# Graph attention and mixture kernel: how the table of edge counts is built from 36 columns of edges at a time

## The chip, the cores and the metric

The kernel runs on one core of a Trainium2 chip. The metric is the device time of one execution in microseconds, the median of several runs. PE is the matrix engine (TensorE), DVE the vector engine, ACT the scalar engine, POOL is GpSimd and SP the engine whose queue issues the DMAs.

## The reference, cut to what matters

There are 1250 nodes and 41250 edges, sorted by their destination. Two layers of graph attention with a residual are followed by a soft mixture of experts. Only the first part matters here:

```
e     = leaky_relu(a_src[src] + a_dst[dst])        # for each edge and head
alpha = softmax of e over the edges of one dst
out   = segment_sum(alpha * h[src], dst)            # 8 heads, then relu
```

The kernel doesn't gather edges. It counts how often each edge (dst, src) occurs, `count[dst, src]`, takes the logarithm of the counts once, and does the attention of each head as a dense one over all sources: `exp(e + ln count)`, normalised by row. So the reference's sums over edges become a 1250 x 1250 table and ordinary matrix products.

## The kernel before, in words

The work is a chain of blocks, each ended by a barrier of all engines. Three of them matter here.

`constants` fills identity, iota and others by POOL.

`first_stage` normalises x, makes h and its attention values (matrix products, 10 tiles of 128 nodes), and finds for each of the 10 tiles of destinations which columns of 128 edges belong to it (`bounds_of_tiles`). Then comes the counting, from line 683 on: for each destination tile `j` a loop over groups of `GROUP` = 36 columns, which with this data runs once for each tile, so ten groups in all. A group has 6 pieces (`b`) of 6 columns (`i`). For each column of 128 edges two one-hot matrices are needed:

- `one_dst`, 128 edges x 128 destinations of this tile, the stationary operand. ACT makes 33 of the 36 (line 782, `apart` = |iota - dst| column by column; line 787, `one_dst` = relu(1 - apart) for a whole piece), DVE the other 3 (line 616).
- `one_src`, 128 edges x 625 sources, the moving operand. Each column counts both halves of the sources at once, since an edge into the upper half is worth `RADIX` = 6144 instead of 1. DVE makes all 36 (line 618).

PE multiplies them into a PSUM accumulator (line 876, two products of 512 and 113 columns for each column of edges). A ring of three pieces couples the engines: DVE and ACT wait for `free` before they write piece b, PE waits for `src_ready`, `dst_ready` and `own_ready`.

The accumulator of a group is unpacked in the middle of the next group. ACT's `round_off` (lines 741 and 745) finds the upper count, `above`, ahead of its piece 3; DVE's `unpack` (lines 627, 629, 632) follows ahead of DVE's piece 3 and adds both halves to `number`. After the group of tile j, ACT takes `log(j - 1)` (line 753) into the one buffer `lns`, for which it waits until DVE's `finish(j - 2)` (line 637) has read the logarithms before. DVE does after the group of tile j: `second_weights` (line 600, for j from 1 to 8), `finish(j - 2)`, and `clear` (line 641), a memset of the `number` buffer that the tile after needs. Three clears stand ahead of the first group as well.

`attend_heads` works through 80 steps (8 heads x 10 tiles) of softmax (ACT, DVE, POOL), transposition and product with h (PE). The product is divided by the softmax's sum. The sums stand in a column and are needed along a row, so `turn_inverse` (lines 951 to 961) has SP write the inverses to DRAM (line 954) and read them back spread over all partitions (line 960), for each of 24 chunks; DVE's `divide` (line 1056) waits for it.

Of the kernel before, what the change touches and what calls it, by code (L numbers as in the profile page):

```python
# [24 lines left out]
F32 = mybir.dt.float32  # L25
F16 = mybir.dt.float16
# [4 lines left out]
ds = bass.ds  # L31
# [207 lines left out]
def constants(nc, mem, sem):  # L239
# [4 lines left out]
    one = mem("one", [P, 1], F32)  # L244
    eps = mem("eps", [P, 1], F32)
# [4 lines left out]
    with nc.Block() as block:  # L250

        @block.gpsimd
        def _(eng):
            eng.memset(ident[:, :], 0.0).then_inc(filled, 1)
            eng.memset(picks[:, :, :], 0.0).then_inc(filled, 1)
            eng.memset(one[:, :], 1.0).then_inc(made, 1)
            eng.memset(eps[:, :], 1e-5).then_inc(made, 1)
# [11 lines left out]
            eng.wait_ge(made, 7)  # L269

    return {"ident": ident, "picks": picks, "one": one, "eps": eps, "none": none, "iota": iota, "zeros": zeros}


def first_stage(nc, mem, early, sem, const, rows, edges, w1t, att1, w2t, att2, bias, h, nad, a_rows, s_row, in_s,
# [13 lines left out]
    ON_DVE = (1, 0, 1, 0, 1, 0)  # L288
    ETP = ET + GROUP
    MOST = NT * -(-ET // GROUP)  # L290
    assert len(ON_DVE) == PIECES and PIECES % RING == 0
# [17 lines left out]
    lns = mem("lns", [P, N], F32)  # L309
    rounded = mem("rounded", [P, HALF], F32)  # L310
# [27 lines left out]
    dst = mem("dst", [P, ETP], F32)  # L338
# [3 lines left out]
    down = mem("down", [P, ET], F16)  # L342
    tiles = mem("tiles", [P, NT], F16)
# [8 lines left out]
    minus_dst = mem("minus_dst", [P, ETP], F32)  # L352
# [15 lines left out]
    row_ready, bounds_ready, minus_ready, levels = (  # L368
        sem("fs_row"), sem("fs_bounds"), sem("fs_minus"), sem("fs_levels"))
    src_ready, apart_ready, dst_ready, own_ready, free = (  # L370
        sem("fs_src"), sem("fs_apart"), sem("fs_dst"), sem("fs_own"), sem("fs_free"))
# [6 lines left out]
    with nc.psum_tensor("fs", [P, 8, BANK], F32) as banks, nc.Block() as block:  # L378
# [26 lines left out]
        def place(b, i):  # L405


            return ((b + 1) % RING) * PIECE + i

# [53 lines left out]
        def _(eng):  # L463
            eng.memset(level[:, :], LEVEL[0]).then_inc(levels, 1)
# [8 lines left out]
            eng.wait_ge(levels, 2)  # L473

        @block.vector
        def _(eng):
            full = [P, NT, ET]

            def tiles_of_edges():
                eng.memset(src[:, ET:ETP], float(NO_NODE)).then_inc(pads, 1)  # L480
                eng.memset(minus_dst[:, ET:ETP], -float(NO_NODE)).then_inc(pads, 1)
# [21 lines left out]
            def nodes_of_edges():  # L503
# [3 lines left out]
                eng.wait_ge(pads, 4)  # L507
                eng.tensor_scalar(upper[:, :], src[:, 0:ET], float(HALF), None, ALU.is_ge).then_inc(casts, 1)
                eng.tensor_scalar(minus_dst[:, 0:ET], dst[:, 0:ET], -1.0, None, ALU.mult).then_inc(minus_ready, 1)
# [4 lines left out]
                                         ALU.mult, ALU.add).then_inc(casts, 1)  # L514

# [106 lines left out]
            def unpack(g, tile):  # L622
# [3 lines left out]
                eng.wait_ge(above_ready, g + 2)  # L626
                eng.scalar_tensor_tensor(rest[:, :], above[:, :], -RADIX, counts(g + 2), ALU.mult, ALU.add)\
# [7 lines left out]
            def finish(j):  # L635
                eng.wait_ge(ln_ready, j + 1)
                eng.scalar_tensor_tensor(ln_c[:, j, 0:N], lns[:, :], NONE_TIMES, lns[:, :],
                                         ALU.mult, ALU.min).then_inc(out_ready, 1)

            def clear(tile):  # L640
                eng.memset(number[:, tile, :], 0.0).then_inc(cleared, 1)
# [41 lines left out]
            for tile in range(3):  # L683
                clear(tile)
            eng.wait_ge(cleared, 3)
            eng.memset(number[:, 0, 0:1], 0.0).then_inc(number_ready, 2)
            eng.wait_ge(casts, 7)
            for j, first, last, shift in spans(eng, True):
                with eng.Fori(first, last) as g:
                    at = first_column(g, shift)  # L690
# [17 lines left out]
                if 2 <= j < NT - 1:  # L708
                    clear((j - 2) % 3)
# [1394 lines left out]
```

## Time and profile before

| what | us |
|---|---|
| median of 3 runs | 1834.65 (1834.17 to 1835.0) |
| the profiled execution's own time | 1835.22 |
| its span, first to last instruction | 1833.4 |
| PE busy | 1634.2 (89%) |
| DVE busy | 1113.2 (61%) |
| ACT busy | 840.0 (46%) |
| POOL busy | 264.2 (14%) |

The counting lies between 106 and 340 us of the span. All times below are us from the span's start, unless they are durations. In a timeline row the columns are start, duration, engine, line, operation, output and inputs, and in square brackets the idle time of the engine before it with what ended it; x5 means five merged instructions.

### The profile page before, as it was taken

The numbers are of one execution on the slowest core, as the hardware profiler recorded it, in microseconds if no ns is written. First come the engines' busy times: TensorE is split into PE (matmuls) and PEld (weight loads), VectorE is DVE, ScalarE is ACT, GpSimd is POOL, SyncE is SP. The second block draws the span as 40 slices with busy tenths as digits, with TensorE's granted clock in tenths as the row PEclk, the third lists the DMA queues.
The fourth block names the chain that finished last, engine by engine and source line by source line (L and its number), as shares of the span: only waits on it lengthen the run. The fifth ranks groups of instructions, "written<-read, shape, count | busy, mean of one in ns | idle before, by whom it ended". The sixth has DMA issues, their size and how long they took to land. (4 is left out here: it accounts for less than half of the span.)

```text
span 1833.4 us, 27161 instructions
## 1 busy us (share of the span) xinstructions
PE 1634.2 (89%) x9537; PEld 956.7 (52%) x9537; DVE 1113.2 (61%) x1853; ACT 840.0 (46%) x1298; POOL 264.2 (14%) x118
## 2 busy tenths in 40 slices
PE   6877665499999989999998999999999969998999
PEld 3433222266656546545553566555565636665555
DVE  7989888689999746332232555555555556665301
ACT  2268777688888638211111333333333335554200
POOL 0000000577878423000000000000000000000000
PEclk9988888699999989999998999999999989999999
DMA  4001000012212240211001111221112225441111
GB/s 168 18 27 48 19 18 10 1 35 48 34 30 36 19 149 1 83 64 35 35 18 36 65 65 64 68 68 68 68 68 68 68 98 176 148 147 30 61 62 49
DMA packets 49747, 108.57 MB, mean 59 GB/s; under 512 B 16638, under 2 KB 18776, under 8 KB 49532
## 3 DMA queue, kind: packets, MB, share of 16 engines
q1 hardware_dynamic: 49596, 107.38, 19.1%
q8 instruction: 49, 0.80, 0.2%
q14 instruction: 38, 0.31, 0.1%
q10 hardware_dynamic: 64, 0.08, 0.0%
HBM read 79.02 MB, written 28.43 MB: 59 GB/s over the span
## 5 line engine op out<-in xcount | busy, mean ns | idle before, releaser
L977 POOL TENSOR_TENSOR base<-s_row,ln_c 128x1250 f32<-128x1250 f32 x80 | 227.6, 2847 | 54.3 <-DVE top L1032 52.9
L876 PE MATMUL fs<-one_src,one_dst 128*128 128x512 f16 x720 | 132.3, 348 | 79.5 <-DVE one_src L618 41.1
L99 PE MATMUL di_l<-x2t_hi,ph_hi 128*128 128x512 f16 (+1 forms) x576 | 196.6, 341 | 5.2 <-POOL p L1594 3.8
L100 PE MATMUL di_l<-x2t_lo,ph_hi 128*128 128x512 f16 (+1 forms) x576 | 196.6, 341 | 0.0
L101 PE MATMUL di_l<-x2t_hi,ph_lo 128*128 128x512 f16 (+1 forms) x576 | 196.4, 341 | 0.0
L1101 PE MATMUL at_o<-pt,h 128*128 128x384 f32 (+1 forms) x480 | 185.9, 525 | 0.0
L876 PEld LDWEIGHTS fs<-one_src,one_dst 128*128 128x128 f16 x720 | 62.0, 113 | 148.6 <-ACT one_dst L787 75.5
L1088 PE MATMUL at_t<-ident,q 128*128 128x128 f32 x800 | 107.4, 283 | 35.7 <-ACT q L1011 35.0
L1088 PEld LDWEIGHTS at_t<-ident,q 128*128 128x128 f32 x800 | 92.2, 145 | 80.1 <-ACT q L1011 71.1
L1653 DVE SCALAR_TENSOR_TENSOR pt_lo<-di_t,pt_hi 128x1280 f16<-128x1280 f32 x32 | 47.7, 1492 | 140.6 <-ACT pt_hi L1607 140.6
L99 PE MATMUL co_c<-ps_hi,hid_hi 128*128 128x305 f16 (+1 forms) x384 | 114.8, 299 | 20.5 <-DVE ps_lo L1896 19.8
L618 DVE TENSOR_SCALAR one_src<-iota,src,worth 128x625 f16<-128x625 f16 x360 | 130.3, 437 | 3.0 <-issue 3.0
L987 ACT ACTIVATE at_r<-s_row,nad 128x1250 f32<-128x1250 f32 x80 | 104.5, 1307 | 37.7 <-DVE top L1032 36.6
L1032 DVE CUSTOM_DVE_ANT_0 q<-at_r,base 128x1250 f32<-128x1250 f32 x80 | 115.8, 1448 | 5.3 <-POOL base L977 3.6
L100 PE MATMUL co_c<-ps_lo,hid_hi 128*128 128x305 f16 (+1 forms) x384 | 114.6, 299 | 0.0
L101 PE MATMUL co_c<-ps_hi,hid_lo 128*128 128x305 f16 (+1 forms) x384 | 114.5, 298 | 0.0
L1101 PEld LDWEIGHTS at_o<-pt,h 128*128 128x128 f32 x480 | 86.0, 192 | 54.5 <-issue 23.8
L1041 DVE COPY pt<-at_t 128x512 f32<-128x512 f32 x160 | 103.1, 685 | 18.6 <-PE at_t L1088 17.3
L782 ACT ACTIVATE apart<-iota,minus_dst 128x128 f16<-128x128 f16 x330 | 102.2, 386 | 11.3 <-PE fs L876 8.7
L1011 ACT ACTIVATE q<-q,neg_top 128x1250 f32<-128x1250 f32 x80 | 105.9, 1324 | 0.8 <-DVE neg_top L1035 0.8
L99 PE MATMUL di_h<-xw,pt_hi 128*128 (+1 forms) x320 | 104.3, 326 | 1.8 <-DVE pt_lo L1653 1.8
L100 PE MATMUL di_h<-xw,pt_hi 128*128 (+1 forms) x320 | 104.3, 326 | 0.0
(271 smaller groups left out, 3305.4 us busy)
## 6 DMA issues: line engine op xcount, KB each, us to landing
logits_t<-lg SPq DMA_DIRECT2D x32, 625.0 KB, 3.6
logits_in<-logits_t SPq DMA_DIRECT2D x32, 625.0 KB, 4.7
phf<-in_phi SPq DMA_DIRECT2D x32, 384.0 KB, 3.9
w2f<-in_w2t SPq DMA_DIRECT2D x16, 384.0 KB, 3.6
s_row<-a_rows SPq DMA_DIRECT2D x9, 640.0 KB, 5.7
ew1f<-in_fw SPq DMA_DIRECT2D x6, 768.0 KB, 4.9
wf<-in_fw SPq DMA_DIRECT2D x12, 384.0 KB, 5.0
xs<-in_x SPq DMA_DIRECT2D x10, 384.0 KB, 4.2
```

The source lines that it names most:

```text
L99: eng.matmul(out, lh, rh, start=first, stop=False, skip_group_check=True)
L100: eng.matmul(out, lh, rl, start=False, stop=False, skip_group_check=True)
L101: return eng.matmul(out, ll, rh, start=False, stop=last, skip_group_check=True)
L618: eng.tensor_scalar(one_src[:, place(b, i), 0:HALF], const["iota"][:, 0:HALF], src[:, ds(col, 1)], worth[:, ds(col, 1)], ALU.is_equal, ALU ...
L876: mm = eng.matmul(counts(g)[:, a:a + n], one_dst[:, place(b, i), :], one_src[:, place(b, i), a:a + n], start=False, stop=b == PIECES - 1 a ...
L977: eng.tensor_tensor(base[:, k % 2, 0:N], s_row[:, head % 2, 0:N], ln_c[:, j, 0:N], ALU.add)\
L987: eng.activation(rp[:, 0:N], s_row[:, head % 2, 0:N], ACT.Relu, bias=nad[:, k:k + 1], scale=-0.8).then_inc(relu_ready, 1)
L1011: eng.activation(q[:, k % RING, 0:N], q[:, k % RING, 0:N], ACT.Exp, bias=neg_top[:, k:k + 1], accum_out=den[:, k:k + 1]).then_inc(p_ready, 1)
L1032: eng.tensor_tensor_reduce(q[:, k % RING, 0:N], rp[:, 0:N], base[:, k % 2, 0:N], 1.0, -MASK / 2, ALU.add, ALU.max, top[:, k:k + 1]).then_i ...
L1041: eng.tensor_copy(pt[:, k % NT, b * (BANK // P):(b + 1) * (BANK // P), :] .rearrange("p t n -> p (t n)"), tp[:, b * BANK:(b + 1) * BANK]). ...
L1088: mm = eng.transpose(tp[:, t * P:(t + 1) * P], q[:, k % RING, t * P:(t + 1) * P], const["ident"][:, :])
L1101: mm = eng.matmul(op[:, g % 2, 0:n * P], h[:, head, t, :], pt[:, a:a + n, t, :], start=t == 0, stop=t == NT - 1, skip_group_check=True)
```

## The change

Counting: DVE makes all of `one_dst`, six columns in one instruction. `one_dst` is laid out `[P, ring, 128 destinations, 6 columns]`, so that a comparison of a constant `spread` (the destination's number, repeated six times) with six entries of `from_tile` fills a piece; PE then reads each column's stationary matrix with a step of 6 elements. `from_tile` is the destination less the tile's start, one small DVE instruction for each group. Of the 36 `one_src` columns of a group ACT makes 10 (`ON_ACT`), each by two instructions over 625 elements, |iota - src| and relu(worth - worth * apart); DVE makes the other 26. ACT's `round_off` moves from piece 3 to piece 2 and DVE's `unpack` from piece 3 to piece 4. `lns` has two buffers. The clears leave DVE: POOL does the first three during the products ahead, ACT the others, after the logarithm, as a Copy with scale 0.

Attention: for the last of the 24 chunks the inverse sums are spread by DVE, PE and ACT (a diagonal matrix multiplied by ones) instead of by SP's way through DRAM.

```diff
+    ones = mem("ones", [P, P], F32)                    # constants, filled by POOL
-    ON_DVE = (1, 0, 1, 0, 1, 0)
+    ON_ACT = (2, 2, 1, 2, 1, 2)
-    lns = mem("lns", [P, N], F32)
+    lns = mem("lns", [P, 2, N], F32)
-    one_dst = mem("one_dst", [P, RING * PIECE, P], F16)
-    apart = mem("apart", [P, 2, PIECE, P], F16)
+    one_dst = mem("one_dst", [P, RING, P, PIECE], F16)
+    apart = mem("apart", [P, 2, HALF_PADDED], F16)
+    spread = mem("spread", [P, P, PIECE], F16)
+    from_tile = mem("from_tile", [P, GROUP], F16)
...
+            eng.wait_ge(casts, 7)                          # POOL
+            for tile in range(3):
+                eng.memset(number[:, tile, :], 0.0).then_inc(cleared, 1)
...
-                eng.tensor_scalar(minus_dst[:, 0:ET], dst[:, 0:ET], -1.0, None, ALU.mult).then_inc(minus_ready, 1)
+                eng.tensor_scalar(minus_src[:, :], src[:, :], -1.0, None, ALU.mult).then_inc(minus_ready, 1)
+                eng.tensor_scalar(minus_worth[:, :], worth[:, :], -1.0, None, ALU.mult).then_inc(minus_ready, 1)
...
             def rows_of(j, g, at, b):                     # DVE
                 eng.wait_ge(free, PIECES * g + b + 1)
-                for i in range(PIECE):
+                eng.tensor_tensor(one_dst[:, ring(b), :, :], spread[:, :, :],
+                                  from_tile[:, b * PIECE:(b + 1) * PIECE].unsqueeze(1)
+                                  .to_broadcast([P, P, PIECE]), ALU.is_equal).then_inc(dst_ready, 1)
+                for i in range(PIECE - ON_ACT[b]):
                     col = at + (b * PIECE + i)
-                    if i >= PIECE - ON_DVE[b]:
-                        eng.tensor_scalar(one_dst[:, place(b, i), :], const["iota"][:, j * P:(j + 1) * P],
-                                          dst[:, ds(col, 1)], None, ALU.is_equal).then_inc(own_ready, 1)
...
-            for tile in range(3):
-                clear(tile)
...
+                    eng.tensor_scalar(from_tile[:, :], dst[:, ds(at, GROUP)], -float(j * P), None, ALU.add)\
+                       .then_inc(from_ready, 1)
-                        if b == PIECES // 2:
+                        if b == 4:
                             eng.wait_ge(cleared, 3 + max(j - 2, 0))
                             unpack(g - 1, tile_of(j, g, first))
...
-                if 2 <= j < NT - 1:
-                    clear((j - 2) % 3)
...
             def log(j, g):                                # ACT
                 eng.wait_ge(number_ready, 2 * g + 4)
-                if j >= 1:
-                    eng.wait_ge(out_ready, j)
+                if j >= 2:
+                    eng.wait_ge(out_ready, j - 1)
...
+                if j + 3 < NT:
+                    eng.wait_ge(ln_ready, j + 1)
+                    eng.activation(number[:, j % 3, :], number[:, j % 3, :], ACT.Copy, scale=0.0)\
+                       .then_inc(cleared, 1)
...
-                        if b == PIECES // 2:
+                        if b == 2:
                             round_off(g - 1)
...
+                        for i in range(PIECE - ON_ACT[b], PIECE):
+                            k = sum(ON_ACT[0:b]) + i - (PIECE - ON_ACT[b])
+                            col = at + (b * PIECE + i)
+                            eng.wait_ge(act_ready, sum(ON_ACT) * g + (k + 1 if k else 2))
+                            eng.activation(apart[:, k % 2, 0:HALF], const["iota"][:, 0:HALF],
+                                           ACT.Abs, bias=minus_src[:, ds(col, 1)]).then_inc(apart_ready, 1)
+                            eng.wait_ge(apart_ready, sum(ON_ACT) * g + k + 1)
+                            eng.activation(one_src[:, place(b, i), 0:HALF], apart[:, k % 2, 0:HALF],
+                                           ACT.Relu, bias=worth[:, ds(col, 1)],
+                                           scale=minus_worth[:, ds(col, 1)]).then_inc(act_ready, 1)
...
-                                mm = eng.matmul(counts(g)[:, a:a + n], one_dst[:, place(b, i), :],
+                                mm = eng.matmul(counts(g)[:, a:a + n], one_dst[:, ring(b), :, i],
...
+                if k == STEPS:                             # attend_heads, ACT
+                    eng.wait_ge(inv_turned, 1)
+                    eng.wait_ge(divided, LAST - 1)
+                    eng.activation(inv[:, LAST % 2, 0:n * P], tp[:, 0:n * P], ACT.Copy).then_inc(inv_read, 1)
...
+                if k == STEPS:                             # DVE, for its n = 3 tiles
+                        eng.tensor_scalar(spread[:, i * P:(i + 1) * P], const["ident"][:, :],
+                                          factor[:, head * NT + a + i:head * NT + a + i + 1], None, ALU.mult)\
...
+                if k == STEPS + 1:                         # PE
+                        mm = eng.matmul(tp[:, i * P:(i + 1) * P], const["ones"][:, :], spread[:, i * P:(i + 1) * P],
+                                        start=True, stop=True)
```

## Rows read from the trace of the kernel before

**Rows 1.** One destination tile by windows: us busy and count by engine, PEclk, DMA.
```profile
197.70:220.20 22.50, 13.61 (x75) 6.65 (x75) 19.45 (x49) 17.64 (x43) 0.00 (x0) 0.80 0.06 19
```

**Rows 2.** Waits from 117 to 329 us: who for whom, total us, times, longest.
```profile
ACT lns L753 <- DVE ln_c L637: 31.1, 7, 4.5
DVE rest L627 <- ACT above L745: 20.3, 8, 3.1
```

**Rows 3.** Timeline of one destination tile, DVE and ACT.
```profile
220.01 1.57 ACT L782 ACTIVATE apart<-iota,minus_dst 128x128 f16<-128x128 f16 x5
...
221.47 4.34 DVE L618 TENSOR_SCALAR one_src<-iota,src,worth 128x625 f16<-128x625 f16 x12
221.61 0.83 ACT L787 ACTIVATE one_dst<-apart,one 128x640 f16<-128x640 f16 x1
...
227.38 0.67 ACT L741 ACTIVATE rounded<-fs 128x625 f32 x1
...
228.81 1.84 ACT L782 ACTIVATE apart<-iota,minus_dst 128x128 f16<-128x128 f16 x6
229.13 0.81 DVE L627 SCALAR_TENSOR_TENSOR rest<-above,fs 128x625 f32<-128x625 f32 x1 [2.82 <-ACT above L745]
...
231.30 3.98 DVE L618 TENSOR_SCALAR one_src<-iota,src,worth 128x625 f16<-128x625 f16 x11
...
237.82 0.95 DVE L600 CUSTOM_DVE_ANT_0 unread<-w2f,attb 128x768 f16<-128x768 f32 x1
...
241.13 1.34 ACT L753 ACTIVATE lns<-number,none 128x1250 f32<-128x1250 f32 x1 [4.47 <-DVE ln_c L637]
```

**Rows 4.** Groups of ACT instructions by form: busy us and mean ns, idle before.
```profile
L782 ACT ACTIVATE apart<-iota,minus_dst 128x128 f16<-128x128 f16 x330 | 102.2, 386 | 11.3 <-PE fs L876 8.7 <-issue 1.8 <-PE fs L857 0.4
L787 ACT ACTIVATE one_dst<-apart,one 128x640 f16<-128x640 f16 x30 | 24.8, 828 | 1.0
L745 ACT ACTIVATE above<-rounded 128x625 f32<-128x625 f32 x11 | 8.0, 726 | 1.4
```

**Rows 5.** DVE two-input instructions on f16 (lines 491, 496): ns min/median/max.
```profile
L491 DVE TENSOR_TENSOR within<-dst_tile,tiles x1: 3532/3532/3532, 26.8 to 26.8; 128x3240 f16<-128x3240 f16 x1
L496 DVE TENSOR_TENSOR ranks<-within,up x1: 1794/1794/1794, 37.8 to 37.8; 128x3240 f16<-128x3240 f16 x1
```

**Rows 6.** Loads of the stationary operand, lines 876 (f16) and 1101 (f32).
```profile
L876 PEld LDWEIGHTS fs<-one_src,one_dst x720: 95/98/152, 117.0 to 329.0; 128*128 128x128 f16 x180
L1101 PEld LDWEIGHTS at_o<-pt,h x480: 190/190/338, 363.7 to 639.6; 128*128 128x128 f32 x160
```

**Rows 7.** Timeline of the start of the counting.
```profile
106.33 1.57 ACT L782 ACTIVATE apart<-iota,minus_dst 128x128 f16<-128x128 f16 x5 [1.43 <-issue]
...
107.26 2.29 DVE L590 TENSOR_REDUCE a_all<-weighted 128x16 f32<-128x2048 f32 x1
...
111.56 0.78 PE L852 MATMUL fs<-level,minus_level 128*128 128x512 f16 x4
...
115.67 1.86 DVE L618 TENSOR_SCALAR one_src<-iota,src,worth 128x625 f16<-128x625 f16 x5 [2.00 <-issue]
```

**Rows 8.** Timeline of the end of the counting and the start of the next block.
```profile
329.88 1.34 ACT L753 ACTIVATE lns<-number,none 128x1250 f32<-128x1250 f32 x1 [2.68 <-DVE ln_c L637]
...
332.86 0.81 DVE L627 SCALAR_TENSOR_TENSOR rest<-above,fs 128x625 f32<-128x625 f32 x1 [3.08 <-ACT above L745]
...
336.57 1.34 ACT L753 ACTIVATE lns<-number,none 128x1250 f32<-128x1250 f32 x1 [3.93 <-DVE ln_c L637]
...
339.93 0.21 ACT L1004 ACTIVATE bias_act<-bias_col 128x8 f32<-128x8 f32 x1 [2.02 <-PEq L378]
```

**Rows 9.** Timeline of the end of the attention over the heads.
```profile
629.24 11.13 PE L1101 MATMUL at_o<-pt,h 128*128 128x384 f32 x34
...
640.50 0.32 SPq L960 DMA_DIRECT2D inv<-inv_rows  x1
...
644.97 0.57 DVE L1056 TENSOR_TENSOR at_o<-at_o,inv 128x384 f32<-128x384 f32 x1 [3.60 <-DMA inv<-inv_rows]
```

More of the change, by code:

```diff
@@ L268, in _ @@
                               channel_multiplier=0).then_inc(made, 1)
-            eng.wait_ge(made, 7)
-    return {"ident": ident, "picks": picks, "one": one, "eps": eps, "none": none, "iota": iota, "zeros": zeros}
+            eng.wait_ge(made, 8)
+    return {"ident": ident, "picks": picks, "one": one, "ones": ones, "eps": eps, "none": none, "iota": iota, "zeros": zeros}
 def first_stage(nc, mem, early, sem, const, rows, edges, w1t, att1, w2t, att2, bias, h, nad, a_rows, s_row, in_s,
@@ L408, in place, with ring @@
             return ((b + 1) % RING) * PIECE + i
+        def ring(b):
+            return (b + 1) % RING
         def tile_of(j, g, first):
@@ L463, in _ @@
         def _(eng):
+            eng.iota(spread[:, :, :], [[1, P], [0, PIECE]], base=0, channel_multiplier=0,
+                     allow_small_or_imprecise_dtypes=True).then_inc(levels, 1)
             eng.memset(level[:, :], LEVEL[0]).then_inc(levels, 1)
@@ L636, in finish @@
                 eng.wait_ge(ln_ready, j + 1)
-                eng.scalar_tensor_tensor(ln_c[:, j, 0:N], lns[:, :], NONE_TIMES, lns[:, :],
+                eng.scalar_tensor_tensor(ln_c[:, j, 0:N], lns[:, j % 2, :], NONE_TIMES, lns[:, j % 2, :],
                                          ALU.mult, ALU.min).then_inc(out_ready, 1)
-            def clear(tile):
-                eng.memset(number[:, tile, :], 0.0).then_inc(cleared, 1)
             def low_w1(k):
@@ L681, in _ @@
                     bounds_of_tiles()
-            for tile in range(3):
-                clear(tile)
-            eng.wait_ge(cleared, 3)
-            eng.memset(number[:, 0, 0:1], 0.0).then_inc(number_ready, 2)
             eng.wait_ge(casts, 7)
+            eng.wait_ge(levels, 3)
+            eng.memset(from_tile[:, 0:1], 0.0).then_inc(dst_ready, 1)
             for j, first, last, shift in spans(eng, True):
@@ L770, in _ @@
                     deviation(t + 3)
-            eng.wait_ge(minus_ready, 1)
+            eng.wait_ge(minus_ready, 2)
+            eng.activation(apart[:, 0, 0:1], const["one"][:, 0:1], ACT.Copy).then_inc(act_ready, 2)
             for j, first, last, shift in spans(eng, True):
@@ L776, in _ @@
                     for b in range(PIECES):
-                        if b == PIECES // 2:
+                        if b == 2:
                             round_off(g - 1)
                         eng.wait_ge(free, PIECES * g + b + 1)
-                        n = PIECE - ON_DVE[b]
-                        for i in range(n):
-                            eng.activation(apart[:, b % 2, i, :], const["iota"][:, j * P:(j + 1) * P],
-                                           ACT.Abs, bias=minus_dst[:, ds(at + (b * PIECE + i), 1)])\
-                               .then_inc(apart_ready, 1)
-                        eng.wait_ge(apart_ready, (GROUP - sum(ON_DVE)) * g
-                                    + (PIECE * (b + 1) - sum(ON_DVE[0:b + 1])))
-                        eng.activation(one_dst[:, place(b, 0):place(b, n), :], apart[:, b % 2, 0:n, :],
-                                       ACT.Relu, bias=const["one"][:, 0:1], scale=-1.0).then_inc(dst_ready, 1)
+                        for i in range(PIECE - ON_ACT[b], PIECE):
[8 more added lines that the diff above has]
+                                           scale=minus_worth[:, ds(col, 1)]).then_inc(act_ready, 1)
                 if j == 0:
@@ L846, in _ @@
             eng.wait_ge(h_read, NT - 1)
[L847 removed]
+            eng.wait_ge(levels, 3)
             eng.wait_ge(bounds_ready, 2)
```

78 lines of the change are left out of this document (54 added, 24 removed).

## The prediction

> **What bounds the kernel now.** I read the page first for the busy shares (PE 89% over the span), which mislead here: the change lies in a stretch in which PE has gaps. So the windows of one destination tile come next [rows 1]. A tile takes 22.5 us, PE is busy for 13.6 of them at a granted clock of 0.80 (between its two levels, 1.2 and 2.4 GHz), DVE for 19.5 and ACT for 17.6. No engine is full, so two of them wait for each other in turn. The waits name them [rows 2]: ACT's logarithm waits 31.1 us for DVE's `finish` in 7 tiles, and DVE's `unpack` waits 20.3 us for ACT's `above`. The timeline shows one round [rows 3]. DVE ends `second_weights` and `finish` 241.13 - 0.10 - 237.82 = 3.2 us after the start of the former; only then may ACT take the logarithm, after 4.47 us of idleness, since `lns` is one buffer. ACT so starts the next tile's `one_dst` late and reaches `round_off` late, and DVE stands idle for 2.82 us ahead of `unpack`. The tile is a ring over both engines: ACT's work of 22.5 - 4.5 = 18.0 us and 4.5 us of DVE.
>
> **ACT after the change.** The prices are [rows 4]. An activation of 128 columns takes 386 ns and one of 640 columns 828, both with a bias read per partition, so 0.863 ns a column, and 386 + 497 x 0.863 = 815 ns for 625 columns. Without such an operand 625 columns take 726 ns [rows 4], so an operand costs about 89. The new |iota - src| has one (815 ns); the new relu has two, bias and scale; no row has two, so it lies between 815 and, with the price of the first paid again, 904. I take 904, as the first operand is the nearest row. Between instructions: five in 1.57 us [rows 3] is (1.57 - 0.386) / 4 = 296 ns from start to start, so neighbours that don't depend overlap by 90 ns. A dependent one starts 221.61 - 221.58 = 0.03 us after the end of what it needs, that of `apart` and `one_dst` [rows 3]. `round_off`, two dependent instructions with one more wait, takes 228.81 - 227.38 = 1.43 us, which leaves 1.43 - 0.67 - 0.73 + 0.09 = 0.12 between them. The new pair is built like `apart` and `one_dst`: 0.815 + 0.03 + 0.904 - 0.09 = 1.66 us. Bounds: 1.57 if the second operand is free, 1.76 if each pair has the gap of 0.12.
>
> A tile on ACT is then 10 x 1.66 = 16.6, `round_off` 1.43, the logarithm 1.34 - 0.09 = 1.25, the clear (0.726 + 625 x 0.000863 = 1.27 us, dependent on the logarithm, so 1.27 + 0.03 - 0.09 = 1.2) and 0.1 for the loop's end: 20.6 us. The 33 + 6 instructions that made `one_dst` are gone. The clear is 1.2 us that ACT didn't have.
>
> **DVE after the change.** A `one_src` costs 4.34 / 12 = 0.36 us [rows 3], 26 of them 9.4. The comparison has 768 elements. Two rows bracket it [rows 5]: 3240 elements took 1794 ns where the repeated input runs along its last dimension (0.52 ns an element and 0.11), and 3532 where one input stands still along it (1.04 and 0.16). In the new comparison both inputs run along the last dimension, of 6 elements, and repeat over the one before, as in the first of these rows, though with an inner run of 324 there and 6 here. So 0.51 us, 0.42 net of the overlap, 2.5 for six; by the other row 0.87 net and 5.2. `VectorE: DVE Perf Modes` of the Trainium skill, section "Mode 2×_1P", asks for 16-bit operands with a step of one and says nothing of a long run; by it the first row holds; the two rows agree with it so far, and no row has a run of 6. With 0.4 for `from_tile` and its waits (at most a `one_src`, 0.44), `unpack` 231.30 - 229.13 = 2.2 and the 3.2 above, DVE's tile is 17.7 us (20.4 by the other row). Either way it is below ACT's 20.6. The comparisons, and the clear and the three `one_dst` that leave DVE, therefore lie beside ACT's work and count for nothing in the steady state; if ACT were faster, DVE's 17.7 would be next.
>
> **The waits.** ACT's logarithm now waits for a `finish` one tile further back, done some 20 us before. `round_off` stands behind four pairs, 6.6 us into ACT's tile, so `above` is there after 8.1. DVE reaches `unpack` after 0.4 + 4 x 0.42 + 17 x 0.36 = 8.2 us of its own; behind the waiting `unpack` are its pieces 4 and 5, which PE needs only when ACT's pairs of them are done, 14.7 and 18.0 us into the tile. ACT itself waits only for `free`: for its piece 3, at 6.6 + 1.4 + 1.7 = 9.7 us, PE must have done piece 0, whose last pair was ready at 3.3. PE needs 625 columns for each column of edges, 0.52 us at 1.2 GHz and 0.26 at 2.4, 18.8 or 9.4 us a tile, so 3.1 us a piece at most. It keeps up at either level, and its clock matters only after the last pair. `round_off`'s and `unpack`'s new waits for `number_ready` are for an unpack a tile earlier: nothing.
>
> **The stationary operand** is read with a step of 12 bytes. No row has such a load; the nearest take 98 ns (f16) and 190 (f32) [rows 6]. I take 98 to 190: at 190 ns the loads add at most 0.1 us to each column at 1.2 GHz, 36 x 0.62 = 22 us, at 2.4 GHz 36 x 0.40 = 14.5, and the busier PE gets the higher level for part of the tile, so still nothing but up to 0.6 us at the end.
> `SBUF — State Buffer` of the skill, "Specifications", speaks against the change: lines are of 16 bytes and want two hits each for full bandwidth. A step of 12 bytes has 1.3 hits. It gives no price; were it the ratio 2 / 1.33, a load would by my estimate take 0.15 us, which ACT's tile still covers. The last rival has its extreme.
>
> **The walk.** ACT starts on the pairs at 106.33 [rows 7] as now, plus 0.3 for two more small DVE instructions in the stage ahead, which I charge in full (each at most 0.44), and 0.1 for a fill of 128 columns in `constants`: 106.7. DVE's three clears and the 2.00 us of issue behind them [rows 7] leave the path: DVE can begin at 107.26 + 2.29 = 109.6 instead of 115.67, PE at 111.56 + 0.78 = 112.3, so neither holds ACT, whose piece 2 is due at 106.7 + 8.1. Tile 0 ends on ACT at 106.7 + 18.0, and the read of h adds up to 1.3: 126.0. Tiles 1 to 7 at 20.6 end at 270.2, tile 8 without a clear at 289.6, tile 9's pairs at 307.6. PE's last piece takes 1.6 to 3.1 more: 310.0. Now from `round_off` on: before, it could start 1.25 after the logarithm of 329.88, at 331.12, and the next block began at 339.93, 8.8 us later [rows 8]. In these, the logarithm of the last tile waited 336.57 - 335.10 = 1.5 for a `finish`, which two buffers remove: 7.3. The next block begins at 317.3 instead of 339.9, 22.6 us earlier.
>
> **The end of the attention.** Before, the last chunk's product was done at 629.24 + 11.13 = 640.4, but the last inverses came at 644.97, for SP issued their load only at 640.50 [rows 9]. After, PE carries three more f32 products of 128 columns in this stretch. Its 34 instructions in 11.13 us are 0.33 each with 384 columns; six with 128 columns lie between a third of that and all of it, 0.65 to 2.0 us, and I take 1.2, as a load of 190 ns each can't be hidden [rows 6]. The division starts at 641.6, 3.4 us earlier. DVE's three small products and ACT's copy stand while PE works on the chunks before. What is late next is PE's product itself.
>
> **Sum.** 22.6 + 3.4 = 26.0 from the profiled execution's 1835.2 is 1809.2; the median of the runs lies 0.6 lower: 1808.6, so 1809.
>
> **Rivals.** (1) The forecast: ACT's pairs set the pace, 1809; chance 0.72. Its own bounds: pairs of 1.57 or 1.76 move 100 of them by -9 or +10, so 1800 to 1819. For it speaks that each length is from a row of the same engine and type.
> (2) DVE sets the pace, chance 0.13. If short runs cost the comparison its double rate, DVE's tile is 20.4, as long as ACT's, and each wait of one on the other adds: 0.6 us a tile for ten tiles, 1815. The start and end gains stay. Against it stands the first row of [rows 5].
> (3) ACT pays more for a dependent pair or for finding its addresses, chance 0.09: a whole 0.2 us for each of 100 pairs, 1829. For it: each pair now has three addresses taken from a register; the 2.00 us of issue in [rows 7] show that an engine's sequencer can be the slow part. Against: `apart` and DVE's `one_src` ran with such addresses at 0.30 and 0.36.
> (4) On the other side, chance 0.06: PE's strided loads. The load isn't hidden beside a product of 113 columns. The change loses once a tile takes 22.5 + 7/10 = 23.2 us (the 7 us being won at both ends), so once a column takes 0.64: a load of 0.21 us more than now at 1.2 GHz, or 0.38 at 2.4. The longest load in the rows is 0.338 [rows 6]; with it added at 1.2 GHz the tile is 36 x (0.52 + 0.24) = 27.4 us, ten of them 49 us more than now less 7, so 1877. Against it: PE has 8.9 us of gaps a tile now and is still granted 0.80 [rows 1]; without gaps it should be granted no less.
> That the edit doesn't work as told (ACT still waiting for DVE) would show as 1 us a tile and lies within (2)'s region.
>
> **Chances and range.** Measurement tells 0.2% (3.7 us) from no change. (1) to (3) are all faster: 0.93; 0.02 for the stretch between 1831 and 1838, which only a mild form of (4) reaches; slower 0.05. The range is 1800 to 1823: the bounds of (1), all of (2) with the ACT bound on top of it; (3) and (4), 0.15, stay outside.
>
> **What would show it.** Right: a tile of about 20.6 us in the windows; ACT over 19 us busy in it and without idle time of a microsecond; pairs of 0.82 and 0.90 us; no row of `log` waiting for `finish`; the comparison at 0.51 us; the counting's block ending near 317; the last `divide` waiting for PE and no DMA. Wrong: a comparison near 0.96; a relu above 1 us, or gaps ahead of `apart`; PE's load above 0.2 us with both others waiting for `free`; idle time of ACT ahead of `round_off`, which would mean that PE comes late.

## The result, and the profile after

| | before | after |
|---|---|---|
| median of 4 runs each, us | 1834.41 (1833.85 to 1835.0) | 1823.41 (1822.06 to 1824.34) |
| the profiled execution's own time | 1835.22 | 1823.05 |
| its span | 1833.4 | 1821.3 |
| one destination tile | 22.50 | 21.78 |
| first pair (or `apart`) of ACT starts | 106.33 | 109.40 |
| the attention's block begins | 339.93 | 332.61 |
| the step behind the attention begins | 649.19 | 637.24 |

The ratio is 0.9939 (95% interval 0.9922 to 0.9957): faster by 11.0 us, where 26 were forecast. Of the 12.1 us between the two spans 7.3 come from the counting and 4.6 from the attention; what follows takes 1184.2 us before and 1184.1 after. The shares of the page, each with the engine's busy us, its part of the span and its instructions:

```profile
PE 1635.9 (90%) x9543; PEld 962.7 (53%) x9543; DVE 1094.6 (60%) x1786; ACT 860.8 (47%) x1117; POOL 270.6 (15%) x124
```

The windows of three neighbouring destination tiles of the changed kernel, with the columns of [rows 1]:

```profile
197.46:219.22 21.76, 13.31 (x76) 6.85 (x75) 17.63 (x42) 20.06 (x24) 0.00 (x0) 0.91 0.06 19
219.22:241.00 21.78, 15.34 (x74) 7.18 (x73) 17.66 (x42) 20.07 (x25) 0.00 (x0) 0.74 0.07 20
241.00:262.78 21.78, 13.46 (x81) 7.08 (x79) 17.65 (x42) 20.07 (x24) 0.00 (x0) 0.96 0.06 18
```

The ring over two engines is gone. The tile takes 21.8 us whether PE is granted 0.74 or 0.96, DVE is busy for 17.65 and ACT for 20.07. The rest of ACT's time isn't a wait for another engine, as its waits between 100 and 325 us show (who for whom, total us, times, longest):

```profile
ACT apart L807 <- issue: 3.5, 8, 1.4
ACT apart L807 <- PE fs L902: 1.2, 1, 1.2
```

No row of the logarithm waiting for `ln_c` is left [rows 2]. So ACT sets the pace, as forecast, and its tile is 1.2 us longer than the 20.6 of the forecast. Where that lies is in ACT's timeline, one pair and a tile's end:

```profile
199.23 0.80 ACT L807 ACTIVATE apart<-iota,minus_src 128x625 f16<-128x625 f16 x1
...
200.17 0.91 ACT L810 ACTIVATE one_src<-apart,worth,minus_worth 128x625 f16<-128x625 f16 x1
200.98 0.81 ACT L807 ACTIVATE apart<-iota,minus_src 128x625 f16<-128x625 f16 x1
...
216.36 1.32 ACT L772 ACTIVATE lns<-number,none 128x1250 f32<-128x1250 f32 x1
...
217.71 1.25 ACT L776 ACTIVATE number<-number 128x1250 f32<-128x1250 f32 x1
...
219.22 0.82 ACT L807 ACTIVATE apart<-iota,minus_src 128x625 f16<-128x625 f16 x1 [0.26 <-issue]
```

From one `apart` to the next are 200.98 - 199.23 = 1.75 us. Both durations are as forecast (0.80 and 0.91 for 0.815 and 0.904), and so is the overlap (200.17 + 0.91 - 200.98 = 0.10). The relu, however, starts 200.17 - 199.23 - 0.80 = 0.14 us after its input is ready, where the forecast had 0.03. No row calls these gaps idle time: they are below what the views report, so a hundred of them stand in no list of waits. From the logarithm to the next tile's first `apart` are 2.86 us, where 1.25 + 1.2 + 0.1 = 2.55 had been put.

The groups of ACT's pair and of DVE's comparison between 100 and 330 us (busy us and mean ns, idle before), and PE's loads of the stationary operand (ns min/median/max):

```profile
L810 ACT ACTIVATE one_src<-apart,worth,minus_worth 128x625 f16<-128x625 f16 x100 | 91.1, 911 | 13.7
L807 ACT ACTIVATE apart<-iota,minus_src 128x625 f16<-128x625 f16 x100 | 80.6, 806 | 4.8 <-issue 3.5 <-PE fs L902 1.2
L634 DVE TENSOR_TENSOR one_dst<-spread,from_tile 128x768 f16<-128x768 f16 x60 | 33.1, 552 | 10.2 <-PE fs L902 9.8
```

```profile
L902 PEld LDWEIGHTS fs<-one_src,one_dst x720: 124/125/153, 115.3 to 324.1; 128*128 128x128 f16 x180
```

The comparison takes 552 ns and the strided load 125. The comparison is near the cheap end of its bounds (0.51 us) and the load in the lower third of 98 to 190 ns, and the run with the plain layout below shows that neither is on the path.

### The profile page after: what moved, and what is told of

It reads as the page before. It is cut to its first block and busy times, and to the rows that moved or that the text cites. A ratio compares the mean times of both kernels' runs of the same rounds, so it can differ in the third digit from the quotient of the medians.

```text
span 1821.3 us, 26819 instructions
## 1 busy us (share of the span) xinstructions
PE 1635.9 (90%) x9543; PEld 962.7 (53%) x9543; DVE 1094.6 (60%) x1786; ACT 860.8 (47%) x1117; POOL 270.6 (15%) x124
## 5 line engine op out<-in xcount | busy, mean ns | idle before, releaser
L902 PEld LDWEIGHTS fs<-one_src,one_dst 128*128 128x128 f16 x720 | 67.0, 132 | 130.5 <-ACT one_src L810 80.4
L101 PE MATMUL di_h<-xw,pt_lo 128*128 (+1 forms) x320 | 104.3, 326 | 0.0
L810 ACT ACTIVATE one_src<-apart,worth,minus_worth 128x625 f16<-128x625 f16 x100 | 91.1, 911 | 13.7
```

Source lines behind the costliest of these rows:

```text
L101: return eng.matmul(out, ll, rh, start=False, stop=last, skip_group_check=True)
L810: eng.activation(one_src[:, place(b, i), 0:HALF], apart[:, k % 2, 0:HALF], ACT.Relu, bias=worth[:, ds(col, 1)], scale=minus_worth[:, ds(co ...
L902: mm = eng.matmul(counts(g)[:, a:a + n], one_dst[:, ring(b), :, i], one_src[:, place(b, i), a:a + n], start=False, stop=b == PIECES - 1 an ...
```

## The experiments

Ratios are to the kernel before on the same chip. A "pair" is the time from one `apart` to the next within a piece, and "block" is the start of the attention's block, 332.6 in the changed kernel. Unless said otherwise an experiment is the changed kernel with the one edit shown.

**The relu's gap.** If the pair's extra time is the wait of the relu for its own `apart`, work in between hides it.

```diff
+                            if k + 1 < sum(ON_ACT):
+                                far(g, at, k + 1)      # |iota - src| of the next column, three apart buffers
                             eng.wait_ge(apart_ready, sum(ON_ACT) * g + k + 1)
-                            eng.activation(one_src[...], apart[:, k % 2, 0:HALF], ACT.Relu, ...)
+                            eng.activation(one_src[...], apart[k % 3][:, 0:HALF], ACT.Relu, ...)
```

> Changed kernel, but ACT issues the |iota - src| of the next column before the relu of this one (three apart buffers), so that no relu depends on the instruction just ahead of it. Theory A (ACT's dependent pairs set the tile's pace; a pair costs 0.80 + 0.14 + 0.91 - 0.09 = 1.76 us because the relu waits 0.14 us for a result just written and loses the overlap of 0.09): the pair falls to 0.71 + 0.82 = 1.53 us, the tile from 21.8 to 19.5, the whole from 1823 to 1801. Theory B (the sequencer, which has three register addresses to find for each pair, sets the pair): the gaps stay, 1820 or more. Theory C (DVE and ACT hold each other through the ring): less than half of A's gain, and ACT idle ahead of its pieces.

Measured: 1797.9 us, ratio 0.9796 (0.978 to 0.9813). ACT's timeline in it and the window of a tile:

```profile
188.57 0.90 ACT L823 ACTIVATE one_src<-apart_c,worth,minus_worth 128x625 f16<-128x625 f16 x1
189.37 0.81 ACT L788 ACTIVATE apart_b<-iota,minus_src 128x625 f16<-128x625 f16 x1
190.07 0.90 ACT L823 ACTIVATE one_src<-apart_a,worth,minus_worth 128x625 f16<-128x625 f16 x1
```

```profile
187.14:206.42 19.28, 14.08 (x75) 7.15 (x75) 17.55 (x42) 18.96 (x25) 0.00 (x0) 0.82 0.07 22
```

Both instructions now overlap their neighbour by 0.10 us, the pair is 190.07 - 188.57 = 1.50, and the tile is 2.50 us shorter, ten times 0.25. The block begins at 307.3, 25.3 us earlier, of which 1.3 are an earlier start of the pairs in that execution (108.05 for 109.40); the time falls by 25.5, a little more than the 22 that were expected. So all of ACT's time in the counting is on the path.

**What the gap consists of.** The relu with one operand per partition less, and the one that is left from a constant column:

```diff
-                                           ACT.Relu, bias=worth[:, ds(col, 1)],
-                                           scale=minus_worth[:, ds(col, 1)]).then_inc(act_ready, 1)
+                                           ACT.Relu, bias=const["one"][:, 0:1], scale=-1.0).then_inc(act_ready, 1)
```

> Changed kernel with the relu of ACT's columns as relu(1 - apart), bias a constant column and scale a number: it leaves out the factor that marks an edge into the upper half, so ACT's columns are counted as if in the lower half. It measures what the two operands addressed by a register cost. If the 0.14 us ahead of the relu come from fetching such operands after the wait: relu 0.82 us, gap 0.03 as for apart and one_dst before, pair 1.56, tile 19.8, 1803. If they are the time until a result of 625 columns can be read: gap 0.14, pair 1.67, tile 20.9, 1814.

Measured: 1804.69 us, ratio 0.984 (0.9825 to 0.9856).

```profile
197.29 0.81 ACT L807 ACTIVATE apart<-iota,minus_src 128x625 f16<-128x625 f16 x1
198.13 0.82 ACT L810 ACTIVATE one_src<-apart,one 128x625 f16<-128x625 f16 x1
198.85 0.80 ACT L807 ACTIVATE apart<-iota,minus_src 128x625 f16<-128x625 f16 x1
```

The pair is 1.56: the relu is 0.09 shorter, and the gap has shrunk from 0.14 to 0.03. That changes two things at once, the number of operands and where their addresses come from, so the next one keeps both operands and fixes the addresses:

```diff
-                                           ACT.Relu, bias=worth[:, ds(col, 1)],
-                                           scale=minus_worth[:, ds(col, 1)]).then_inc(act_ready, 1)
+                                           ACT.Relu, bias=const["one"][:, 0:1],
+                                           scale=const["eps"][:, 0:1]).then_inc(act_ready, 1)
```

> Changed kernel with the relu's bias and scale both read per partition, but from constant columns, not from addresses in registers; it leaves out the value of ACT's columns (what they count is meaningless), to measure one cost. If the gap ahead of the relu comes from the addresses in registers: relu 0.91, gap 0.04, pair 1.66, the length the prediction took. If it comes from the second per-partition operand: gap 0.14, pair 1.76.

Measured: 1814.51 us, one execution only, so the reading rests on the lengths in its trace.

```profile
196.13 0.81 ACT L807 ACTIVATE apart<-iota,minus_src 128x625 f16<-128x625 f16 x1
196.97 0.92 ACT L810 ACTIVATE one_src<-apart,one,eps 128x625 f16<-128x625 f16 x1
197.78 0.81 ACT L807 ACTIVATE apart<-iota,minus_src 128x625 f16<-128x625 f16 x1
```

Two operands with fixed addresses make a relu of 0.92, a gap of 196.97 - 196.13 - 0.81 = 0.03 and a pair of 1.65, a hundredth from the 1.66 of the forecast. So the second operand costs the 0.09 that was put for it, and the 0.10 that was missing goes with operands whose address is taken from a register, in an instruction that waits for the one just ahead. `ScalarE: Activation LUTs` of the Trainium skill, "What ACT_TABLE_LOAD costs", says that each pointer operand adds about 93 ns and that neighbours overlap by about as much; the trace agrees (820 to 911 ns, overlap 0.10).

The rows of ACT's sequencer (ACTq, as PEq is PE's) show a part of the gap. In the changed kernel it runs a short instruction on registers for each relu, between the end of the first `apart` (109.40 + 0.82 = 110.22) and the relu:

```profile
L810 ACTq FUSED_REGOPS  x100: 37/43/43, 110.3 to 323.0; - x100
L810 ACT ACTIVATE one_src<-apart,worth,minus_worth x100: 909/911/915, 110.4 to 323.1; 128x625 f16<-128x625 f16 x100
```

With two fixed addresses the same line has the activation alone. With another `apart` in between, the first register instruction stands 0.6 us ahead of its relu (at 109.5), beside a running activation:

```profile
L810 ACT ACTIVATE one_src<-apart,one,eps x100: 912/914/918, 108.9 to 312.2; 128x625 f16<-128x625 f16 x100
L823 ACTq FUSED_REGOPS  x100: 37/43/43, 108.9 to 297.1; - x100
```

Its 0.04 us are a part of the 0.11 by which the gap shrinks; what the rest is, no row shows.

**The start.** The first clears moved from POOL to ACT, into its gap in the first stage.

```diff
-            eng.wait_ge(casts, 7)                          # POOL
-            for tile in range(3):
-                eng.memset(number[:, tile, :], 0.0).then_inc(cleared, 1)
...
+                if t == 6:                                 # ACT, first stage
+                    eng.wait_ge(casts, 7)
+                    for tile in range(3):
+                        eng.activation(number[:, tile, :], const["iota"][:, 0:N], ACT.Copy, scale=0.0)\
+                           .then_inc(cleared, 1)
```

> Changed kernel, but the first three clears of number are made by ACT in a gap of the stage ahead instead of by POOL at 80 us. Theory A (POOL's memsets hold up DVE's minus_worth and weigh by 1.4 us, PE then idles 2 us and is granted 1.2 GHz for a while, 1.4 us more): minus_worth falls from 1.37 to 0.35 us, PE's wait at 88 us from 2.0 to 0.5, the counting starts 2.6 us earlier, 1820.5. Rival (the two DVE instructions that were added cost it): 1823 as before.

Measured: 1820.77 us, ratio 0.9924 (0.9904 to 0.9945), which the intervals don't tell from the changed kernel. The traces show what the fills cost. First the changed kernel's timeline, then the same instruction in this one:

```profile
79.87 0.35 DVE L534 TENSOR_SCALAR minus_src<-src 128x360 f32<-128x360 f32 x1
79.98 3.67 POOL L491 MEMSET number<- 128x1250 f32 x3 [72.16 <-DVE src L531]
80.13 1.37 DVE L535 TENSOR_SCALAR minus_worth<-worth 128x360 f32<-128x360 f32 x1
81.42 0.94 DVE L599 TENSOR_TENSOR xt_lo<-fs,xt_hi 128x768 f16<-128x768 f32 x1
```

```profile
L530 DVE TENSOR_SCALAR minus_worth<-worth x1: 342/342/342, 80.2 to 80.2; 128x360 f32<-128x360 f32 x1
```

While POOL fills, `minus_worth` takes 1.37 us instead of 0.34. A third of the three fills is 1.2 us, so the first is over at about 81.2, and `minus_worth` ends 0.3 us later. The `xt_lo` behind it takes 0.94 us beside the next fill, as its ten instances do everywhere (0.94 to 0.96). This is the lock of which `SBUF — State Buffer` of the Trainium skill tells in "Who interferes with whom": a tensor_scalar in a mode that uses both of DVE's port pairs stands back for any POOL instruction that was first, and an instruction outside these modes, with at most one input in SBUF, doesn't (one input of `xt_lo` is in PSUM). The trace agrees on both, 1.03 us lost and none.

ACT starts the pairs at 107.60 here, 1.8 us earlier where 2.6 were expected. The changed kernel's 109.40 is not all POOL's doing: PE's granted clock between 90 and 95 us was 0.77 in that trace. Over the traces of all kernels that have POOL's clears, ACT starts at 109.4 to 109.5 in the three with a granted clock of 0.74 to 0.77 there, and at 108.0 to 108.9 in the six with 1.00. So of the 2.7 us that the start is late, about 1.3 are PE's clock in that one execution, and 0.5 to 1 the fills. The three kernels without the fills still start at 107.2 to 107.6, 0.5 to 0.9 us after the forecast's 106.7. ACT's instruction that opens the count of pairs (0.20 us) stands there without a term in the sum; the rest of it is open. What brings the lower clock stays open: PE waits 1.99 us for `normed` in each of the three, but in three of the six too.

**Fewer pairs on ACT.**

```diff
-    ON_ACT = (2, 2, 1, 2, 1, 2)
+    ON_ACT = (1, 2, 1, 2, 1, 1)
```

> Changed kernel with ON_ACT = (1, 2, 1, 2, 1, 1): 8 columns on ACT, 28 on DVE. Theory A (ACT sets the pace, 1.76 us a pair, DVE has 3 us to spare a tile): ACT's tile 21.8 - 3.5 = 18.3, DVE's 17.9 + 0.7 = 18.6; DVE takes over, a tile of 18.7 to 19.7, the whole 1794 to 1803. Theory C (the ring of both engines sets the pace): a gain of 10 us at most, 1813 or more.

Measured: 1789.98 us, ratio 0.9755 (0.9739 to 0.9772).

```profile
204.60:222.90 18.30, 13.14 (x76) 7.10 (x76) 18.27 (x44) 16.87 (x21) 0.00 (x0) 0.91 0.07 22
```

The tile is 3.48 us shorter, two pairs of 1.75, and DVE, with 28 rows, is busy for 18.27 of its 18.30 us. ACT's own sum, eight pairs of 1.755 and 4.2 beside them, is 18.2, so both engines are full. The time is 4 us below the 1794 to 1803 that were expected, as DVE's tile came out at 18.3 and not at 18.7 or more. The ten of the change are two too many: ACT's 21.8 stood against DVE's 17.65.

**The last inverses the old way**, through DRAM by SP; the three small products and their copies removed.

```diff
-                    if head * CHUNK + c < LAST:
-                        turn_inverse(head * CHUNK + c)
+                    turn_inverse(head * CHUNK + c)
```

> Changed kernel with the last inverse denominators read back through DRAM by SP, as before the change. The part is worth what the two traces differ by between the start of the attention and the next block, 309.3 - 304.6 = 4.6 us: 1828. If the difference lay elsewhere in the attention: 1823 to 1825.

Measured: 1829.3 us, ratio 0.9968 (0.9955 to 0.998). From the block's start to the step behind the attention it takes 643.63 - 331.50 = 312.1 us, against 637.24 - 332.61 = 304.6. That trace is of the slowest of six executions (1832.2), and the kernel before, with the same way through DRAM, took 309.3; so the traces give 4.6 to 7.5 us for this part. The median is 5.9 above that of the changed kernel, which ran on another chip, where 4.6 were expected. First its timeline, then the changed kernel's:

```profile
624.31 0.32 SPq L989 DMA_DIRECT2D inv<-inv_rows  x1
...
626.49 0.37 SPq L983 DMA_DIRECT2D inv_rows<-factor  x1
634.17 0.57 DVE L1085 TENSOR_TENSOR at_o<-at_o,inv 128x384 f32<-128x384 f32 x1 [7.12 <-DMA inv<-inv_rows]
...
635.57 0.32 SPq L989 DMA_DIRECT2D inv<-inv_rows  x1
...
639.70 0.57 DVE L1085 TENSOR_TENSOR at_o<-at_o,inv 128x384 f32<-128x384 f32 x1 [3.19 <-DMA inv<-inv_rows]
```

```profile
621.86 0.32 SPq L989 DMA_DIRECT2D inv<-inv_rows  x1
...
626.50 0.57 DVE L1096 TENSOR_TENSOR at_o<-at_o,inv 128x384 f32<-128x384 f32 x1 [1.12 <-DMA inv<-inv_rows]
...
633.31 0.57 DVE L1096 TENSOR_TENSOR at_o<-at_o,inv 128x384 f32<-128x384 f32 x1 [4.47 <-PE at_o L1156]
```

The last chunk but one has its inverses 4.6 us after their load is issued in the changed kernel, and 9.9 us after it here, where the last chunk's store is issued 2.2 us behind that load. The kernel before has the same delay: load at 628.70, store at 631.19, division at 639.02. A store behind a load doesn't delay it by itself, though. These are the landings of the changed kernel's 23 loads:

```profile
DMA to landing us min/median/max: 3.3/4.6/10.8
```

Five of them (issued at 433.38, 469.04, 540.25, 575.20 and 586.37) have the next chunk's store 1.9 to 2.5 us behind them and land within 4.3 to 5.0 us; the one issued at 610.43, with its store 2.5 us behind, takes the 10.8. So without the last chunk's way through DRAM the load ahead of it lands in time, and why it is late otherwise stays open.

**One log buffer.**

```diff
-                if j >= 2:
-                    eng.wait_ge(out_ready, j - 1)
-                eng.activation(lns[:, j % 2, :], number[:, j % 3, :], ACT.Ln, bias=const["none"][:, 0:1],
+                if j >= 1:
+                    eng.wait_ge(out_ready, j)
+                eng.activation(lns[:, 0, :], number[:, j % 3, :], ACT.Ln, bias=const["none"][:, 0:1],
```

> Changed kernel with one lns buffer and the old wait for the finish just before. Theory A (in the changed kernel DVE runs ahead of ACT, its finish ends at 215.8 where the logarithm is due at 216.4, so the second buffer removes no wait in the tiles): the tile stays 21.8, only the last logarithm waits 1.5 us, 1823 to 1826. Theory D (the second buffer is what removed the 4.5 us a tile, as the prediction has it): 4 us or so come back in each of 8 tiles, 1850 and more.

Measured: 1826.96 us, ratio 0.9959 (0.9947 to 0.9971). The waits between 100 and 325 us have one row for it:

```profile
ACT lns L772 <- DVE ln_c L659: 1.7, 1, 1.7
```

That one is in the last tile, and the last logarithm of all comes 1.5 us later too. The block begins at 335.0, although this execution starts the pairs at 108.1: from there it takes 227.0 us, against 223.2 in the changed kernel, 3.8 more. The median is 3.6 above, 1 us over the range expected. In the tiles before, nothing changes. With the comparison in one instruction and fewer rows to make, DVE is done with `finish` before ACT wants to take the logarithm: in the changed kernel the DVE instruction at 214.36 (`ln_c`, 1.45 us) ends 0.55 us ahead of ACT's logarithm at 216.36.

**A stationary operand without a step**, for which the comparison has one input that stands still along the last dimension.

```diff
-    one_dst = mem("one_dst", [P, RING, P, PIECE], F16)
+    one_dst = mem("one_dst", [P, RING, PIECE, P], F16)
...
-                                mm = eng.matmul(counts(g)[:, a:a + n], one_dst[:, ring(b), :, i],
+                                mm = eng.matmul(counts(g)[:, a:a + n], one_dst[:, ring(b), i, :],
```

> Changed kernel with one_dst laid out column by column, so that PE's load is contiguous, and the comparison has one input that stands still along the last dimension. Theory A (ACT sets the pace, the strided load and DVE's comparison lie beside it): the load falls from 125 to 98 ns, the comparison rises from 552 to about 960 ns, DVE's tile to 20.3, below ACT's 21.8; the whole 1821 to 1826. If the strided load costs time: 1818 or less. If DVE's length counts through the ring: 1828 or more.

Measured: 1823.79 us, ratio 0.9938 (0.992 to 0.9956).

```profile
L903 PEld LDWEIGHTS fs<-one_src,one_dst x720: 94/98/153, 114.7 to 324.2; 128*128 128x128 f16 x180
...
L634 DVE TENSOR_TENSOR one_dst<-iota,from_tile x60: 946/953/960, 112.5 to 318.8; 128x768 f16<-128x768 f16 x60
```

The load is 98 ns again and the comparison 953, near the other end of its bounds. Both prices change and the time doesn't, so neither is on the path while ACT has ten rows.

**Together.** The early `apart` and the clears by ACT, as above, and nine rows on ACT:

```diff
-    ON_ACT = (2, 2, 1, 2, 1, 2)
+    ON_ACT = (1, 2, 1, 2, 1, 2)
```

> Changed kernel with ACT's pairs interleaved as in e1, the first clears on ACT as in e2, and ON_ACT = (1, 2, 1, 2, 1, 2), 9 columns. By theory A each engine's tile is its own sum: ACT 4.2 + 9 x 1.51 = 17.8, DVE 18.2 - 0.36 = 17.8 (28 columns took 18.2 without a gap in e3), so a tile of 17.9 to 18.4 against 18.3 in e3; with 1.6 us from the start 1782 to 1788. If a balanced ring loses to both waits: 1790 and more.

Measured: 1789.42 us, ratio 0.9757 (0.9743 to 0.9771).

```profile
201.31:219.09 17.78, 13.61 (x77) 6.82 (x75) 17.75 (x43) 17.45 (x22) 0.00 (x0) 0.90 0.07 23
```

DVE is busy for 17.75 of 17.78 us and ACT for 17.45: both are full. The block begins at 296.8, yet the time is that of the kernel with only eight rows on ACT, and above the 1782 to 1788 that were expected. Both were run again, on one chip:

> The kernel of e3, for comparison on one chip: tile 18.3, 1790.

> The kernel of e9 on the same chip as e12. Its trace had tiles of 17.8 against 18.3 and a start 1.6 us earlier, though its median was equal. Theory A: 4 to 6 us below e12. Rival: what it wins in the counting is lost later, equal within 2 us.

Measured: 1790.59 (0.9746 to 0.9773) and 1791.32 (0.9753 to 0.9781). The block begins at 302.8 and 296.6, the attention ends at 607.0 and 602.2, and the spans are 1791.4 and 1788.0. Of 6.2 us gained in the counting, about 1.4 go in the attention and 1.4 behind it. The 3.4 that are left in the spans don't show in the medians, whose single runs lie between 1788.5 and 1794.3: the traced execution of the kernel with eight rows is the slowest of its five (1793.18), that of the other the second fastest (1789.88). So the rival of the expectation holds, equal within 2 us, and where the shorter tiles are lost is open. Either version is faster than the changed kernel by 32 to 34 us, and the one-line edit is enough.

## Why the prediction was wrong

The sign and the mechanism were right, and the time wasn't: 1823.4 is 14 us above the forecast and 0.4 above the range. Of the profiled 15.3 us by which the block began late (332.6 for 317.3), the traces give:

| term of the sum | forecast | measured | us late |
|---|---|---|---|
| start of ACT's pairs | 106.7 | 109.40 | 2.7 |
| a pair, 100 of them | 1.66 | 1.755 | 9.5 |
| per tile beside the pairs | 4.0 | 4.2 | 1.9 |
| loading ACT's table before the first logarithm | 0 | 1.28 | 1.3 |
| the rest, above all ACT's one wait for `free` in the second tile | 0 | 1.0 | 1.0 |
| PE behind ACT's last pair | 2.4 | 1.2 | -1.1 |

**The pair** is the step that failed: the forecast let the relu start 0.03 us after its input, and it started 0.14 us after, which made the pair 1.755 us and not 1.66, in each of a hundred. The 0.03 us between dependent instructions was read from `apart` and `one_dst` [rows 3], whose second had a fixed operand; the relu takes two from a register. The text knew a pair of 1.76, as the bound with the gap of `round_off`, and a rival with the price of register addresses, at 0.2 us and a chance of 0.09. It was 0.10 us, so that rival had the mechanism at double the size. That the bound of 1.76 held is luck, as its reason was another: `round_off` has fixed operands, and its own gap in the changed kernel is 205.18 - 204.48 - 0.67 = 0.03. A hundred instructions at 0.1 us are 0.5% of this kernel. The row needed was one with both traits, dependent and addressed by register, and where none exists the middle of the bounds is the better value.

**The start** had a price for the two small DVE instructions and none for what POOL's fills do to them. The three clears were counted as gone from DVE; one of them came back as 1.03 us of DVE's wait in the stage ahead, at a place where DVE feeds PE. PE's clock in that execution is a larger part of this term, and no step of the forecast's.

**The ends of the tiles.** ACT's next `apart` starts 219.22 - 217.71 - 1.25 = 0.26 us after the clear, where the forecast had 0.1 for the loop's end less an overlap of 0.09. It also took the overlap off the logarithm, although the clear behind it depends on it and starts 217.71 - 216.36 - 1.32 = 0.03 after its end. Against that, `round_off` takes 1.33 us and not 1.43. **The table load** stood before the first logarithm already (1.28 us at 149.88), but there each later logarithm waited for `finish`, up to 4.5 us [rows 2], which could take it in. With these waits gone it is on the path:

```profile
149.56 1.28 ACT L772 ACT_TABLE_LOAD   x1
```

Its cover was removed together with the wait, and the sum has no term for it.

**The waits.** That the logarithm would stop waiting was right, its reason only in part: the forecast gave it to the second buffer, and with one buffer the tiles are the same. DVE's shorter tile did it. What the second buffer is worth is 3.8 us at the end, of which the two waits are 1.7 in the last tile and 1.5 behind it, where 1.5 were put.

**DVE** was forecast at 17.7 us a tile and is 17.65, **the strided load** at 98 to 190 ns and is 125, below the 150 estimated from `SBUF — State Buffer` of the Trainium skill, "Specifications", whose direction is right: a step of 12 bytes costs 27 ns over the 98. Rival (2), DVE as the pace, and rival (4), PE's loads, fell. DVE waits 20.2 us for `above` as before [rows 2]:

```profile
DVE rest L649 <- ACT above L764: 20.2, 8, 2.7
```

The forecast had DVE at `unpack` after 8.2 us of its own and `above` ready after 8.1. In truth ACT needs 8.4 us for it (205.91 for a tile begun at 197.46), and DVE starts each tile 3.5 us ahead of ACT (`from_tile` at 215.73, `apart` at 219.22). As DVE has 4 us to spare, this costs nothing.

**The end of the counting**, from `round_off` to the block, was 7.3 by forecast and is 332.61 - 325.21 = 7.4:

```profile
323.99 1.32 ACT L772 ACTIVATE lns<-number,none 128x1250 f32<-128x1250 f32 x1
...
325.21 0.67 ACT L761 ACTIVATE above<-fs 128x625 f32 x1
...
326.97 0.81 DVE L649 SCALAR_TENSOR_TENSOR rest<-above,fs 128x625 f32<-128x625 f32 x1 [1.32 <-ACT above L764]
...
329.25 1.34 ACT L772 ACTIVATE lns<-number,none 128x1250 f32<-128x1250 f32 x1 [2.62 <-DVE number L654]
...
332.61 0.21 ACT L1034 ACTIVATE bias_act<-bias_col 128x8 f32<-128x8 f32 x1 [2.02 <-PEq L388]
```

PE's last products are covered by the logarithm of tile 8, which is why that term came out shorter. **The attention** gave 4.6 us instead of 3.4: PE's three products lengthen its stretch by only 0.2 us (its last product ends 300.7 us into the block, 300.4 before), not by 1.2. What is late next is PE's product, as forecast.

**The range** took the pair's bounds, but nothing for errors that add up beside it; start, table load and loop ends are 6 us, all on the slow side. A sum of many small terms in which forgotten ones can only be positive wants a range that reaches further up.

**Slips in the working** made little difference. The upper bound of the pair is 0.815 + 0.12 + 0.904 - 0.09 = 1.75, not 1.76. The range was to hold all of rival (2) with the ACT bound on top, which is 1815 + 10 = 1825 and not 1823; the measured time lies between the two. The chances of (1) to (3) add up to 0.94, not 0.93. In rival (4) a column of 0.64 us at 1.2 GHz, with 0.52 for the products of which 0.09 stand beside the load, means a load of 0.21 us in all, 0.12 more than now, and not 0.21 more; at 2.4 GHz it is 0.33 more and not 0.38. The measured 125 ns are far from either.

## What to carry to other kernels

When work is spread over two engines, put both engines' tile times side by side and move the split until they are equal: here one line (eight rows for ten) brought another 33 us, three times what the change brought. Price a short dependent instruction by its start-to-start time, with the same kinds of operands and addresses, and put independent work between the two where the count is high. When a wait is removed, look for what it was hiding.

## What the runs showed of the hardware

- A dependent activation with two per-partition operands at addresses from a register starts 0.14 us after its input is ready; with fixed addresses 0.03. With another activation in between, nothing is left of it (pair 1.755, 1.65 and 1.505 us).
- A POOL memset of 1250 f32 columns held up a DVE tensor_scalar of 360 f32 columns that started during it (1.37 us instead of 0.34), and not a tensor_tensor with one input in PSUM (0.94 us).
- A comparison of 768 f16 elements with inner runs of six takes 552 ns; with an input that stands still along the last dimension it takes 953.
- A stationary operand read with a step of 12 bytes takes 125 ns to load, 98 without a step.
- The load that spreads the inverses over the partitions lands 3.3 to 10.8 us after its issue, in the middle 4.6. A small store 1.9 to 2.5 us behind it didn't make it late in five cases of six, and what did in the sixth is open.
